# First expert mixture: tiles 0 and 1 gathered by one joint product of high and low rows, tiles 2 to 5 by a second behind unit 7, and the low rows computed on GpSimd

## The reference, cut to what matters

```python
x = x + _L0_ffn_ref(_layernorm(x, axis=-1), keys, w1, b1, w2, b2, rw, rb)

def _L0_ffn_ref(x, keys, w1, b1, w2, b2, rw, rb):
    E, TOP_K = (16, 4)
    F = 4 * D                                    # 1024
    diff = x[:, :, None, :] - keys
    dist2 = jnp.sum(diff * diff, axis=-1)
    logits = -dist2 + jnp.einsum('bld,ed->ble', x, rw) + rb
    topv, topi = jax.lax.top_k(logits, TOP_K)
    w = jax.nn.softmax(topv, axis=-1)
    hidden = jax.nn.gelu(jnp.einsum('bld,efd->blef', x, w1) + b1, approximate=False)
    exp_out = jnp.einsum('blef,edf->bled', hidden, w2) + b2
    sel = jnp.take_along_axis(exp_out, topi[..., None], axis=2)
    fused = jnp.sum(w[..., None] * sel, axis=2)
    return fused
```

## Time and profile before

| | |
|---|---|
| median of 3 runs | 722.17 us |
| lowest, highest | 721.88, 723.37 us |
| span of the profiled execution | 720.9 us |
| PE, PEld busy | 94%, 77% |
| DVE, ACT, POOL busy | 75%, 57%, 63% |

### The profile page before, as it was taken

The page is one execution under the profiler, slowest core; times in us unless marked ns, Lnnn a source line. Parts: engine busy times, 40 slices in busy tenths (PEclk is TensorE's granted clock), DMA queues, the critical chain, the costliest instruction groups (busy, mean ns, idle before and its releaser), DMA issues.

```text
span 720.9 us, 15536 instructions
## 1 busy us (share of the span) xinstructions
PE 679.9 (94%) x5712; PEld 556.0 (77%) x5712; DVE 540.9 (75%) x1212; ACT 413.8 (57%) x790; POOL 451.1 (63%) x487
## 2 busy tenths in 40 slices
PE   6799999999999979699999999999999899999998
PEld 3577777777777768599999999997457467676787
DVE  5787878787889676167777777763657899999577
ACT  3665756656755652267666666752335886665441
POOL 4748634547486736387999778745413699898130
PEclk9999999999999989799999999999999999999999
DMA  8301101001007474599989999995794520001000
GB/s 342 122 2 60 60 1 58 22 36 59 0 0 307 170 290 193 218 393 405 357 334 335 330 345 342 335 378 185 273 366 150 202 98 0 1 1 45 1 0 30
DMA packets 20365, 123.38 MB, mean 171 GB/s; under 512 B 2304, under 2 KB 6672, under 8 KB 13008
## 3 DMA queue, kind: packets, MB, share of 16 engines
q1 hardware_dynamic: 17376, 114.59, 41.7%
q0 software_dynamic: 2928, 8.00, 3.0%
HBM read 111.77 MB, written 10.81 MB: 170 GB/s over the span
## 4 chain that ended last, share of the span: by engine, by line
PE 80%; DVE 9%; ACT 5%; issue 2%; DMA 2%; another core or an unknown queue 1%; POOL 0%; DVEq 0%; SPq 0%; ACTq 0%; PEldq 0%
PE banks L2263 68%; PE banks L2331 8%; DVE shown L2129 2%; PE banks L2895 2%; DMA ctx_raw<-in_ctxT 1%; ACT probs L1142 1%; DVE negmax_raw L1659 1%; PE banks L2572 1%; ACT banks L1430 1%; DVE banks L2136 1%; DMA table<-in_table 1%; DVE xn L1551 1%; PE banks L2731 0%; POOL rstd L698 0%
## 5 line engine op out<-in xcount | busy, mean ns | idle before, releaser
L2263 PE MATMUL banks<-xT,raw 128*128 128x128 f32 x992 | 151.6, 276 | 0.6 <-DVE xT L1917 0.6
L2263 PEld LDWEIGHTS banks<-xT,raw 128*128 128x128 f32 x992 | 135.0, 192 | 3.4 <-issue 1.3
L970 POOL TENSOR_TENSOR w_lo<-raw,w_hi 128x1024 fp32r<-128x1024 f32 x52 | 122.6, 2383 | 1.6 <-ACT w_hi L1262 1.0
L1293 ACT ACTIVATE banks<-banks,later 128x128 f32<-128x128 f32 x208 | 70.6, 340 | 58.2 <-PE banks L2263 56.9
L1923 DVE CAST mid_hi<-banks 128x128 fp32r<-128x128 f32 x208 | 60.1, 289 | 36.6 <-ACT banks L1293 34.5
L1172 ACT ACTIVATE probsT<-banks 128x512 f32<-128x512 f32 x68 | 40.1, 598 | 74.8 <-PE banks L2331 74.5
L1042 POOL TENSOR_TENSOR inject<-BCbc,drive 128x1024 f32<-128x1024 f32 x31 | 72.8, 2363 | 11.3 <-DVE shown L2129 6.5
L1142 ACT ACTIVATE probs<-banks,negmax 128x1024 f32<-128x1024 f32 x64 | 71.2, 1113 | 11.9 <-DVE negmax L1661 10.0
L1659 DVE TENSOR_REDUCE negmax_raw<-banks 128x1 f32<-128x1024 f32 x64 | 77.5, 1210 | 0.4 <-PE banks L2263 0.3
L2263 PE MATMUL banks<-w_hi,mid_hi 128*128 128x256 f32 x208 | 75.5, 363 | 0.0
L2331 PE MATMUL banks<-table,probs 128*128 128x128 f32 x512 | 69.6, 279 | 0.4 <-DVE probsT L1632 0.4
(11 more groups left out here) (362 smaller groups left out, 1730.5 us busy)
## 6 DMA issues: line engine op xcount, KB each, us to landing
raw<-in_w SPq DMA_DIRECT2D x31, 2048.0 KB, 9.1
ctx_raw<-in_ctxT SPq DMA_DIRECT2D x8, 1024.0 KB, 4.8
ctxT<-in_ctxT SPq DMA_DIRECT2D x4, 2048.0 KB, 9.1
ctxN<-in_ctxN SPq DMA_DIRECT2D x4, 2048.0 KB, 13.6
x_slots<-zero SPq DMA_DIRECT2D x1, 3968.0 KB, 12.5
y_slots<-y_tile POOLq DMA_DIRECT2D x29, 128.0 KB, 7.2
wf<-in_w SPq DMA_DIRECT2D x9, 384.0 KB, 5.4
BCbc<-bc_rows SPq DMA_DIRECT2D x6, 512.0 KB, 6.9
```

Of the source, the lines that this page charges most:

```text
L970: nc.gpsimd.tensor_tensor(w2_lo[i % WB][:, cols], raw[i % WB][:, EW // 2:][:, cols], w2_hi[i % 2][:, cols].bitcast(F32), ALU.subtract).the ...
L1293: nc.scalar.activation(to, held, ACT.Gelu, bias=b1[:, bass.ds(at + u, 1)]).then_inc(gelu_done, 1)
L2263: return nc.tensor.matmul(o, lhsT, rhs, start=start, stop=stop)
```

## The change

- The high and low rows now serve all directly gathered tiles. `xn_lo` is computed on POOL in one instruction over 128 x 1024, behind its four `rstd_of` and ahead of its wait for the slots; the two DVE instructions go.
- `dispatch_first` gathers tiles 0 and 1 jointly: 16 float32r products (high and low) of 256 columns. Its one-hot comes in two halves by token chunk, and PE begins with the first half. Both halves stand in `place_rows` ahead of the slot numbers.
- `dispatch_rest` gathers tiles 2 to 5, and comes at n = 8, behind `down(7)`. HOT is 6, so `turn_rows` starts at tile 6 and the pieces of `x_rows` begin there.
- `turn_spread` goes from units 32 and 36 to 40 and 44, and SP's third `slot_rows` one tile later.
- DVE's order: both copies of `take_rows` for tiles 0 and 1, four one-hots, `owners`, `gates`, `spread_gates`, and then `take_tile(0)`, `take_rows(2)` and so on.

```diff
-HOT, REST_AT = 5, 4
+HOT, PAIR, REST_AT = 6, 2, 8
-SPREAD_AT = tuple(UNITS * i + u for i, u in ((4, 0), (4, 4)))
+SPREAD_AT = tuple(UNITS * i + u for i, u in ((HOT - 1, 0), (HOT - 1, 4)))
...
-        hot = nc.alloc_sbuf_tensor_at("hot", [P, TC, P], F32, offset=hot_at)
-        hot_rest = nc.alloc_sbuf_tensor_at("hot_rest", [P, TC, HOT - 1, P], F32R, offset=hot_at + TC * P * 4)
+        hot = nc.alloc_sbuf_tensor_at("hot", [P, TC, PAIR, P], F32R, offset=hot_at)
+        hot_rest = nc.alloc_sbuf_tensor_at("hot_rest", [P, TC, HOT - PAIR, P], F32R, offset=hot_at + PAIR * TC * P * 4)
...
+        low_rows_ready, low_rows_before = keys_ready, 2
...
-            return 1 if i == 0 else 2 if i < HOT else i - HOT + 3
+            return 1 if i < PAIR else 2 if i < HOT else i - HOT + 3
...
-                if i == PLAIN:
+                if i == PLAIN + 1:
                     sp.wait_ge(spread_turned, share_before + LAST)
                     slot_rows(2)
...
             for t in range(TC):
                 rstd_of(3, t)
 
+            pool.wait_ge(ssq_ready, TC + 1)
+            nc.gpsimd.tensor_tensor(xn_lo[:], xn[:], xn_hi[:].bitcast(F32), ALU.subtract).then_inc(low_rows_ready, 1)
             pool.wait_ge(zeroed, 32)
             pool.wait_ge(slots_ready, 1)
...
+            def one_hot_pair(of):
+
+                here = pos[:, of, 0:PAIR]
+                nc.vector.tensor_tensor(hot[:, of], over(here, P, 3), over(over(inc[:], PAIR, 1), here.shape[1], 1), ALU.is_equal)\
+                    .then_inc(sel_ready, 1)
+
             def one_hot(i):
 
-                to = hot_rest[:, :, i - 1, :] if i else hot[:]
-                nc.vector.tensor_tensor(to, over(pos[:, :, i], P, 2), over(inc[:], TC, 1), ALU.is_equal).then_inc(sel_ready, 1)
-
-            def low_rows(of):
-
-                dve.wait_ge(ssq_ready, TC + 1)
-                nc.vector.tensor_tensor(xn_lo[:, of, :], xn[:, of, :], xn_hi[:, of, :].bitcast(F32), ALU.subtract).then_inc(sel_ready, 1)
+                nc.vector.tensor_tensor(hot_rest[:, :, i - PAIR, :], over(pos[:, :, i], P, 2), over(inc[:], TC, 1), ALU.is_equal)\
+                    .then_inc(sel_ready, 1)
...
-                one_hot(0)
+                one_hot_pair(slice(0, TC // 2))
+                one_hot_pair(slice(TC // 2, TC))
...
             place_rows()
-            low_rows(slice(0, TC // 2))
-            take_rows(0)
-            for i in range(1, HOT):
+            for i in range(PAIR):
+                take_rows(i)
+            for i in range(PAIR, HOT):
                 one_hot(i)
-            low_rows(slice(TC // 2, TC))
             owners()
-            for i in range(PLAIN):
-                take_rows(i + 1)
-                if i == 0:
-                    gates()
-                    spread_gates()
-                if i + 1 < PLAIN:
-                    take_tile(i)
+            gates()
+            spread_gates()
+            for i in range(PLAIN - 1):
+                take_tile(i)
+                take_rows(i + PAIR)
...
             def dispatch_first():
 
-                pe.wait_ge(sel_ready, sel_before + 3)
-                for c in range(DC):
-                    for t in range(TC):
-                        last = mm(pb(TURN_BANK)[:, c * P:(c + 1) * P], xn[:, t, c * P:(c + 1) * P], hot[:, t, :], t == 0, t == TC - 1)
+                pe.wait_ge(low_rows_ready, low_rows_before + 1)
+                width = PAIR * P
+                for t in range(TC):
+                    if t % 2 == 0:
+                        pe.wait_ge(sel_ready, sel_before + 3 + t // 2)
+                    for c in range(DC):
+                        for of in (xn_hi, xn_lo):
+                            last = mm(pb(TURN_BANK)[:, c * width:(c + 1) * width], of[:, t, c * P:(c + 1) * P],
+                                      hot[:, t].rearrange("p i n -> p (i n)"), t == 0 and c == 0 and of is xn_hi,
+                                      t == TC - 1 and c == DC - 1 and of is xn_lo)
                 last.then_inc(rows_turned, 1)
 
             def dispatch_rest():
 
-                pe.wait_ge(sel_ready, sel_before + HOT + 4)
-                pe.wait_ge(xT_ready, 1)
+                pe.wait_ge(sel_ready, sel_before + 4 + HOT - PAIR)
+                pe.wait_ge(xT_ready, PAIR)
```

More of the change, by code:

```diff
@@ L1911, in take_rows @@
                     dve.wait_ge(up_done, UNITS * (i - 1))
-                if 0 < i < HOT:
+                if i < PAIR:
+                    nc.vector.tensor_copy(xT[i][:], pb(TURN_BANK).rearrange("p (c i n) -> p i c n", c=DC, i=PAIR)[:, i]).then_inc(xT_ready, 1)
+                    return
+                if i < HOT:
                     for c in range(DC):
-                        last = nc.vector.tensor_copy(xT[i % 2][:, c, :], pb(REST_BANKS[c])[:, (i - 1) * P:i * P])
+                        last = nc.vector.tensor_copy(xT[i % 2][:, c, :], pb(REST_BANKS[c])[:, (i - PAIR) * P:(i - PAIR + 1) * P])
                     last.then_inc(xT_ready, 1)
@@ L2561, in dispatch_rest @@
                         for of in (xn_hi, xn_lo):
-                            last = mm(pb(REST_BANKS[c])[:, 0:(HOT - 1) * P], of[:, t, c * P:(c + 1) * P],
+                            last = mm(pb(REST_BANKS[c])[:, 0:(HOT - PAIR) * P], of[:, t, c * P:(c + 1) * P],
                                       hot_rest[:, t].rearrange("p i n -> p (i n)"), t == 0 and of is xn_hi, t == TC - 1 and of is xn_lo)
```

## The result

| | before | after |
|---|---|---|
| median of 5 runs, us | 721.88 (721.39 to 723.37) | 724.58 (723.62 to 724.81) |
| profiled execution, us | not given apart | 724.66 |
| its span, us | 720.9 | 722.9 |
| ratio of the times | 1 | 1.0035, 95% interval 1.0023 to 1.0047 |

The change makes the kernel 2.5 us slower than before, by the ratio. I had forecast +0.72 us.

What follows compares the result with a forecast made beforehand. The hold, taken to end with POOL's run of indirect DMAs, was to set when PE goes on; +1.2 + 0.62 - 0.88 - 0.22 = +0.72 us, put on the median of 722.17, gave 722.9 us, range 720.6 to 724.7.

Steps and rivals of the forecast that it cites:

- What bounds the kernel: After the router, about 284 to 297 us: the hold, ending with POOL's indirect DMAs, sets when PE's down(10) starts.
- the hold: Stretch beside POOL's 16 scatters where PE's finished work is seen late by all waiters; forecast to end at 298.6 us.
- Low rows on POOL: DVE's scan `passed` waits beside POOL's subtraction, delaying all behind it on DVE: +1.2 us, bounds 0 and +1.5.
- the row at 690 us: A DVE instruction with two SBUF inputs that took 2.21 us beside a POOL subtraction, against a median of 0.68.
- Second one-hot ahead of the slots: On DVE, two one-hots now precede `slots`: +0.62 us, with scatters from 275.5 us.
- First gather: PE's 16 products take 3.84 us against 3.54, first up about 275.7 us; the +1.5 us is covered by the hold.
- Second gather at unit 8: PE's gather runs 284.0 to 287.8 across the hold's start; PE goes on with down(11), one unit more: -0.88 us.
- rival 3: The hold begins by PE's own count of increments, no unit gained: 723.8 us, up to 725.4 with the restart; chance 0.16.
- The rest: `turn_rows(5)` leaves PE's path, -0.22 us; SP loads expert 5 at about 284 us, worth nothing; other moves cost nothing.
- the restart: Behind the hold PE starts at the 1.2 GHz level, its clock rising some 3.3 us later, as before.

Runs made afterwards that it cites:

- slots_first: V with the second half of the first one-hots made behind the slot numbers, as before the change; 721.34 us, ratio 0.9993.
- quarter_rows_after: The changed kernel with 16 scatters of 64 columns instead of 256, part of the computation left out; 723.64 us, ratio 1.002.
- two_units_apart: V with scatter k waiting for Gelu 2k, 22 at most; 719.80 us, ratio 0.9971.
- low_weights_ahead: two_units_apart with POOL writing the low weights of tile 3 ahead of its last four scatters; 717.82 us, ratio 0.9943.
- V: The changed kernel with ACT writing high rows behind each token tile's square and POOL the low rows in four pieces; 721.23 us, ratio 0.9994.
- rest_at_4: V with the second gather behind unit 3, as before the change; 722.41 us, ratio 1.0016.
- low_on_pool_before: The kernel before with the low rows in one POOL instruction as in the change, nothing else; 724.18 us, ratio 1.0039.

## Why the prediction came out as it did

*What bounds the kernel.* Right, and now shown: without the run of scatters the hold is gone and 9 us with it, and its end follows the last scatter by 3.2 to 3.5 us in six executions. That PE's speed ahead of the hold is worth nothing is not shown: the number of units that it gets behind it counts, 0.88 us each.

*Low rows on POOL.* The size was near (+1.2 forecast, with +1.5 as the upper bound; +1.47 measured at `passed`, of which 1.32 is the wait and 0.15 a later start), the instruction was wrong: I chose the scan with two SBUF inputs, by the row at 690 us, and it was `picked`, with one input, that waited. The Trainium skill, page "SBUF — State Buffer", section "Who interferes with whom", has this case too: a `tensor_scalar` can run in a two-port mode, where its operands allow it, and then contends with GpSimd for the shared pair. The trace agrees: 1.55 us instead of 0.23, with the end 0.09 us behind POOL's; which mode it ran in no trace here shows. I had read the rule for the instruction that I had in mind, not for each one in the window.

*Second one-hot ahead of the slots.* +0.62 forecast; slots less `passed` gave +0.61. The first scatter came at 275.74 (275.5 forecast), the end of the hold at 298.52 (298.6). That the last two agree so well is partly luck: the first scatter was 0.26 us later than forecast, the run of scatters 0.58 us shorter than before, and the group 0.27 us further behind its last one.

*First gather.* 3.77 us and a first up at 275.98 (3.84 and 275.7 forecast). What I had left out is the clock behind it: the 16 records of the first ups took 3.75 us against 2.02 before, at the 1.2 GHz level. The granted clock was 0.50 from 276 to 280 us, where before it was 1.00.

*Second gather at unit 8: the step that failed.* I wrote that all increments up to up(10) are made by 284.0 and that the hold, moved with the scatters, begins at about 286. PE in fact made up(10) only at 286.47, mostly by the slow first ups, and the hold began at 282.96, 7.2 us behind the first scatter and not 10.6. PE had to wait for Gelu 7, the second gather lay wholly inside the hold, PE then stopped for 3.53 us in the middle of up(11) and up(12), which no term of mine had, and it came out with down(9) instead of down(11): two units, 1.76 us. I had counted one as a gain, -0.88, and must now count one as a loss, +0.88. The time is in the range of rival 3 (no unit gained, 723.8 to 725.4), though even that one lost no unit; its reason, PE's own count of increments, is not borne out, since the first late one was up(8), up(6), up(7), up(10), up(8) and up(8) in the six executions of the table. Why the hold began earlier stays open. So the time came out inside the range because the range was 4.1 us wide, and not because the term was right.

*The rest.* The -0.22 stands in the sum above; the restart was shorter by 0.55 us. Expert 5's weights did not load at about 284, as I had it: SP saw tile 0's last down only at 298.56, behind the hold (296.79 before).

In sum, forecast +0.72 with terms 1.2 + 0.62 - 0.88 - 0.22; measured in the spans +2.0 with 1.86 (the later restart, for 1.2 + 0.62) + 0.88 - 0.22 - 0.55.

## What to carry to other kernels

If a long run of indirect DMAs stands beside a busy PE, look whether PE's increments come late, and try to break the run up (here worth 0.3%, and 0.6% with one more move): pace it by the consumer's progress, and then look at what else stands in that queue, because the wait comes back there. Before you move work to GpSimd, list every DVE instruction that can fall into its time, small ones with one input too: 64 columns cost 1.3 us here. And where a stall releases PE, count how many units it has behind it: work that is only shifted ahead of the stall pays by that count alone.

## What the runs showed of the hardware

While POOL issues indirect DMAs 1.27 us apart, the semaphore increments of PE reach their waiters (ACT, DVE, SP) late, singly and mostly 2.4 to 11.3 us apart, and all at once 3.2 to 3.5 us behind the start of the last DMA; PE's own waits for ACT show none of this (in the changed kernel Gelu 7 ends at 288.95 and down(7) starts at 289.00). But late in the hold PE itself can stop within a unit, waiting for nothing that the profile shows: 1.95, 1.13 and 0.45 us in the changed kernel, and the like in slots_first and quarter_rows_after. It is not the bytes (a quarter of them, the same hold). With scatters 1.76 us apart Gelus were at most 0.5 us late, and with four at a time and a wait until they had landed none was late. Four or five in a row at 1.27 us behind such a paced part brought single Gelus 1.1 and 2.1 us late (two_units_apart, low_weights_ahead), two in a row none. When the long hold begins is open: 7.2 us behind the first scatter in the changed kernel and in its variant with a quarter of the bytes, 8.1 in V, 10.3 in rest_at_4, 10.6 in the kernel before, 11 in slots_first, 12 in low_on_pool_before, and no count of PE's increments explains it. That some queue fills up would fit all of this, but no run shows the queue.
